# A cross-attention and mixture-of-experts kernel: expert loop bounds read from the table once, a table of steps of its own for the first batch, and the low half of the context split in two pieces

## The reference, cut to what matters

```python
# x: (8, 512, 256), ctx: (8, 1024, 256); 8 heads of 64, 8 experts, all float32
x = x + tanh(g_xattn) * attention(layernorm(x), ctx)
#   q = x @ Wq; k, v = ctx @ Wk, ctx @ Wv; softmax(q k^T / 8) @ v; @ Wo + bo
h = layernorm(x).reshape(4096, 256)
p = softmax(h @ router.T); top 2 of 8 experts, their weights normalised
keep the 1280 heaviest assignments of each expert, renormalise
x = x + tanh(g_ffn) * sum over kept experts of weight * ((h @ W1) * silu(h @ Wg)) @ W2
```

## Time and profile before

| what | value |
|---|---|
| time, median of 3 runs (lowest to highest) | 1725.2 us (1725.16 to 1726.33) |
| profiled execution, its own time | 1727.69 us |
| its span | 1726.0 us |
| TensorE busy | 1642.6 us, 95% |
| VectorE busy | 1270.0 us, 74% |
| ScalarE busy | 1050.0 us, 61% |
| GpSimd busy | 671.9 us, 39% |
| batch 0, first scores to those of batch 1 | 21.78 to 153.85 us |
| search, TensorE's part (slot 4) | 1145.7 to 1149.0 us |
| experts 1 to 7 | 1196.48 to 1715 us |

### The profile page before, as it was taken

The page is one execution under the profiler, slowest core; times in us unless marked ns, Lnnn a source line. Parts: engine busy times, 40 slices in busy tenths (PEclk is TensorE's granted clock), DMA queues, the critical chain, the costliest instruction groups (busy, mean ns, idle before and its releaser), DMA issues.

```text
span 1726.0 us, 33535 instructions
## 1 busy us (share of the span) xinstructions
PE 1642.6 (95%) x12454; PEld 1494.2 (87%) x12454; DVE 1270.0 (74%) x2595; ACT 1050.0 (61%) x2179; POOL 671.9 (39%) x615
## 2 busy tenths in 40 slices
PE   6999999999999999999999998999999999999997
PEld 4788878887888887888888886889999999999997
DVE  6887888888888888888888878676565556547443
ACT  5776766766767666766676766535454455546443
POOL 3342444444345345245345334423343422232322
PEclk9999999999999999999999999999999999999999
DMA  4200220121121021031030022314423421341212
GB/s 126 124 25 1 85 77 26 64 86 38 35 107 45 17 121 50 13 124 51 13 124 32 20 120 85 135 44 106 114 41 108 111 34 39 97 113 28 38 32 28
DMA packets 60555, 115.49 MB, mean 67 GB/s; under 512 B 6616, under 2 KB 48480, under 8 KB 59776
## 3 DMA queue, kind: packets, MB, share of 16 engines
q1 hardware_dynamic: 37104, 79.24, 13.0%
q0 software_dynamic: 15392, 18.66, 5.9%
q10 hardware_dynamic: 7920, 15.73, 2.6%
HBM read 90.27 MB, written 57.42 MB: 86 GB/s over the span
## 4 chain that ended last, share of the span: by engine, by line
PE 76%; DVE 11%; issue 4%; POOL 3%; ACT 3%; DMA 1%; POOLq 0%; DVEq 0%; SPq 0%; ACTq 0%
PE ring L1207 11%; PE turned L1101 11%; PE ffn L1064 10%; PE ffn L1066 10%; PE ffn L1065 10%; PE scores L1089 9%; DVE neg_max L1888 5%; PE ring L1064 4%; PE ring L1066 3%; PE ring L1065 3%; DVE pt_l L1665 2%; PE ring L1173 1%; PE ring L1175 1%; POOL lists L855 1%; POOL probs L889 1%
## 5 line engine op out<-in xcount | busy, mean ns | idle before, releaser
L889 POOL TENSOR_SCALAR probs<-probs,row_rec 128x1024 f32<-128x1024 f32 x254 | 282.2, 1123 | 478.6 <-DVE row_rec L1991 466.9
L1429 ACT ACTIVATE pt_h<-turned 128x512 fp32r<-128x512 f32 x512 | 279.5, 602 | 209.7 <-PE turned L1101 209.2
L1665 DVE TENSOR_TENSOR pt_l<-turned,pt_h 128x512 fp32r<-128x512 f32 x512 | 331.0, 680 | 7.2 <-ACT pt_h L1429 6.8
L1888 DVE TENSOR_REDUCE neg_max<-scores 128x1 f32<-128x1024 f32 x256 | 301.5, 1218 | 35.7 <-PE scores L1089 35.6
L1101 PE MATMUL turned<-ident,probs 128*128 128x128 f32 x2048 | 281.9, 279 | 30.3 <-DVE pt_l L1665 23.3
L1101 PEld LDWEIGHTS turned<-ident,probs 128*128 128x128 f32 x2048 | 224.2, 141 | 98.4 <-issue 69.9
L1485 ACT ACTIVATE probs<-scores,neg_max 128x1024 f32<-128x1024 f32 x256 | 285.3, 1117 | 14.9 <-DVE neg_max L1888 14.8
L1207 PE MATMUL ring<-pt_h,v_hl 128*128 128x256 f32 x1024 | 261.4, 293 | 0.2
L1207 PE MATMUL ring<-pt_l,v_hl 128*128 128x256 f32 x1024 | 250.9, 283 | 0.0
L2256 DVE TENSOR_TENSOR act_f<-ffn,silu 128x256 f32<-128x256 f32 (+1 forms) x232 | 108.4, 467 | 130.7 <-ACT silu L1599 123.3
L1207 PEld LDWEIGHTS ring<-pt_h,v_hl 128*128 128x128 f32 x1024 | 195.7, 191 | 4.0 <-issue 1.9
(11 more groups left out here) (258 smaller groups left out, 3905.4 us busy)
## 6 DMA issues: line engine op xcount, KB each, us to landing
lists<-pads SPq DMA_DIRECT2D x8, 4160.0 KB
w_raw<-w_t ACTq DMA_DIRECT2D x10, 1024.0 KB, 8.3
e_rows<-lists SPq DMA_DIRECT2D x26, 390.0 KB
ctx_raw<-ctx_t SPq DMA_DIRECT2D x15, 512.0 KB, 3.8
wg_raw<-wg_t ACTq DMA_DIRECT2D x5, 1024.0 KB, 7.8
x_in<-x SPq DMA_DIRECT2D x8, 512.0 KB, 4.0
x_sum<-x SPq DMA_DIRECT2D x8, 512.0 KB, 4.0
out<-x_sum SPq DMA_DIRECT2D x8, 512.0 KB, 2.9
```

Source lines behind the costliest of these rows:

```text
L889: nc.gpsimd.tensor_scalar(probs[:, k, :], probs[:, k, :], row_rec[:, k:k + 1], 1.0, ALU.mult, ALU.mult).then_inc(scaled, 1)
L1429: return nc.scalar.activation(dst, src, ACT.Copy)
L1665: return nc.vector.tensor_tensor(dst, src, hi_part.bitcast(F32), ALU.subtract)
L1888: nc.vector.tensor_reduce(neg_max[:, k:k + 1], scores[:, n % 2, :].rearrange("p (a c) -> p a c", a=2), AX.XY, ALU.max, negate=True).then_i ...
```

## The change

Four edits, in a diff cut to its core.

TensorE no longer loads bounds at each expert. The search loads, right after it has waited for the table, two ends for each of the experts 1 to 7 (14 loads) ahead of the one of the turns; VectorE computes the wide ends (row 2) and a copy of the ends (row 6) in two more small operations. The other engines load as before. `FIRST` has a table of its own, `FIRST_JOBS`, and `FIRST_EARLY` says for each even step how many of the two `low_turned` stand between the two `highest`. GpSimd's `ctx_l` is written as two operations of 128x512 instead of one of 128x1024. `FILL_A` keeps later tiles where they were.

```diff
-FILL_A = 32
+FILL_A = 24
+FIRST_JOBS = {
+    0: [("w", 1, 0), ("k", 1, 0)],
...
+    7: [("k", 2, 0)],
+    8: [("v", 1, 0)],
...
+FIRST_EARLY = {0: 2, 2: 2, 4: 1, 8: 2, 12: 2, 14: 1, 16: 1, 18: 1, 22: 1, 24: 1, 28: 1, 30: 1}
-LOW_BETWEEN = (24, 26, 28, 30)
+LAST_EARLY = {24: 2, 26: 2, 28: 2, 30: 2, UNITS - 1: 2}
...
-FIRST = Body(0, False, True, True, START.end - RING, START)
+FIRST = Body(0, False, True, True, START.end - RING, START, FIRST_JOBS)
...
-                nc.gpsimd.tensor_tensor(ctx_l[:, :, part], ctx_raw[:, :, :],
-                                        ctx_h[:, :, part].bitcast(F32), ALU.subtract)\
-                    .then_inc(ctx_split, 1)
+                for kc in range(KC):
+                    last = nc.gpsimd.tensor_tensor(ctx_l[:, kc, part], ctx_raw[:, kc, :],
+                                                   ctx_h[:, kc, part].bitcast(F32), ALU.subtract)
+                last.then_inc(ctx_split, 1)
...
                     pe.wait_ge(table_done, 1)
+                    for e in range(1, E):
+                        ends.append([pe.value_load(table[0:1, row, e:e + 1], min_val=LEAST_MORE,
+                                                   max_val=MOST_CHUNKS) for row in (2, 6)])
                     turns = pe.value_load(table[0:1, 3, 1:2], min_val=1, max_val=WEIGHT_BITS)
...
-                wides = pe.value_load(table[0:1, 4, ds(e, 1)], min_val=1, max_val=2)
-                chunks = pe.value_load(table[0:1, 0, ds(e, 1)], min_val=1, max_val=T // CHUNK)
-                before = pe.value_load(table[0:1, 1, ds(e, 1)], min_val=0, max_val=MOST_CHUNKS)
+                wide_end, end = ends[e - 1]
...
-                with pe.Fori(0, wides) as j:
-                    whole_chunk(pe.snap(before + j), parity, WT)
-                with pe.Fori(0, chunks) as j:
-                    whole_chunk(pe.snap(before + wides + j), parity, ST)
+                with pe.Fori(start, wide_end) as n:
+                    whole_chunk(n, parity, WT)
+                with pe.Fori(wide_end, end) as n:
+                    whole_chunk(n, parity, ST)
+                return end
...
+                    nc.vector.tensor_tensor(table[:, 2, :], table_f[:, 1, :], table_f[:, 0, :], ALU.subtract)
+                    nc.vector.tensor_copy(table[:, 6, :], table_f[:, 1, :])
```

More of the change, by code:

```diff
@@ L109 @@
 FIRST_VALUES = {0: [("v", 0, 0), ("v", 0, 1)], 1: [("v", 0, 2)], 2: [("v", 0, 3)]}
+FIRST_JOBS = {
+    0: [("w", 1, 0), ("k", 1, 0)],
+    2: [("w", 1, 1)],
+    3: [("k", 1, 1)],
+    4: [("w", 1, 2), ("q", 1, 0)],
+    6: [("w", 1, 3)],
+    7: [("k", 2, 0)],
+    8: [("v", 1, 0)],
+    9: [("v", 1, 1)],
+    10: [("q", 2, 0)],
+    12: [("k", 2, 1)],
+    13: [("h", 0, 0)],
+    14: [("v", 1, 2)],
+    15: [("w", 0, 0)],
+    16: [("w", 0, 1), ("k", 3, 0)],
+    17: [("v", 1, 3)],
+    18: [("h", 1, 0)],
+    19: [("w", 0, 2), ("l", 0, 0)],
+    20: [("k", 3, 1), ("q", 3, 0)],
+    22: [("x", 0, 0)],
+    23: [("w", 0, 3), ("x", 1, 0)],
+    24: [("v", 0, 0), ("k", 0, 0)],
+    26: [("k", 0, 1)],
+    27: [("v", 0, 1), ("r", 0, 0)],
+    28: [("v", 0, 2), ("q", 0, 0)],
+    30: [("v", 0, 3)],
+}
+FIRST_EARLY = {0: 2, 2: 2, 4: 1, 8: 2, 12: 2, 14: 1, 16: 1, 18: 1, 22: 1, 24: 1, 28: 1, 30: 1}
 LN_STEPS = 6
@@ L173, in of @@
     def of(self, b):
-        return Body(b, self.prev, self.own, self.nxt, self.offset, self.before)
+        return Body(b, self.prev, self.own, self.nxt, self.offset, FIRST if b == 1 else self.before)
     def route_from(self):
@@ L319, in build @@
         table_f = tile(moe, "table_f", [P, 7, E])
-        table = tile(moe, "table", [P, 6, E], I32)
+        table = tile(moe, "table", [P, 7, E], I32)
         tile(moe, "rest_of_x_in", [P, FILL_A])
@@ L1238, in _ @@
             batches(pe, run)
+            ends = []
             def search(slot):
@@ L1402, in first_expert, with expert @@
                 down(pe.snap(chunks + EARLY - 1), FC - 1, 0)
[L1404 to L1408 removed]
+                return chunks
+            def expert(e, parity, start):
+                wide_end, end = ends[e - 1]
                 if e == 1:
                     pe.wait_ge(w_split, 2 * PIECES)
[L1412 to L1415 removed]
+                with pe.Fori(start, wide_end) as n:
[3 more added lines that the diff above has]
+                return end
             chunk(0, 0, True)
[L1418 removed]
+            start = first_expert()
             for e in range(1, E):
[L1420 removed]
+                start = expert(e, e % 2, start)
         @block.scalar
@@ L1960, in step @@
                     jobs = body.results(u)
-                    lows = body is LAST and u in LOW_BETWEEN + (UNITS - 1,)
-                    late = [(what, c) for what, c in jobs if lows and what[0] == "r"]
+                    done = 0
+                    if body.own and u >= 2:
+                        done = {FIRST: FIRST_EARLY, LAST: LAST_EARLY}.get(body, {}).get(u, 0)
+                    late = [(what, c) for what, c in jobs if body is LAST and done and what[0] == "r"]
                     jobs = [job for job in jobs if job not in late]
@@ L1969, in step @@
                         highest(b, u)
-                        if lows:
-                            low_turned(b, u - 2, 0)
-                            low_turned(b, u - 2, 1)
+                        for j in range(done):
+                            low_turned(b, u - 2, j)
                         if body is LAST and u == UNITS - 2:
@@ L1995, in step @@
                     between(body, u, 2)
-                    if (body.prev if u < 2 else body.own) and not lows:
+                    if (body.prev if u < 2 else body.own) and done < 1:
                         low_turned(b, u - 2, 0)
-                        between(body, u, 3)
+                    between(body, u, 3)
+                    if (body.prev if u < 2 else body.own) and done < 2:
                         low_turned(b, u - 2, 1)
-                    else:
-                        between(body, u, 3)
                     between(body, u, 4)
```

## The result

The changed kernel takes 1724.0 us (median of 16 runs, 1721.5 to 1725.7) beside 1726.3 for the kernel before on the same chip (median of 16); the ratio of the two is 0.9982, 95% interval 0.9975 to 0.9989: 0.18% or 3.1 us faster (1.9 to 4.3), at the edge of what can be told from no change. I had forecast 1719.4. The profiled execution of the change took 1722.29 us of its own (span 1720.6), 5.4 less than that of before, where my sum said 6.9.

A forecast was written before the change was run, and what follows sets the result against it. TensorE, at work 95% of the span, was taken as the bound, so only its idle time could yield gains. Terms -8.2 + 5.2 + 2.6 + 0.2 - 3.4 - 2.2 gave -5.8 against 1725.2: 1719.4 us, range 1711.5 to 1727.

The forecast's parts named there:

- The loads that go (-8.2): At the first matmul of experts 1 to 7, TensorE's idle time for bound loads should vanish: -8.2 us.
- nothing of the 8.24 us should stay: Claim that all seven issue gaps at experts 1 to 7 end, as one load and the branch are hidden.
- The loads that come (+5.2): In the search, 15 loads in a row at 0.6 us each bring the small matmul 5.2 us later.
- the rival of cheap loads: Loads cost 0.2 us each, so the search hides them, with no clock term: 1711.6 us; chance 0.12.
- The clock (+2.6): After over 8 us of standing still in the search, TensorE runs six microseconds at 1.2 GHz: +2.6 us.
- The table (+0.2): Two more small VectorE operations before `act_f`, for which TensorE waits ahead of the search: +0.2 us.
- Batch 0 (-3.4): New step order and early `low_turned` end TensorE waits in batch 0, less 0.6 for late maxima: -3.4 us.
- the wait of step 9: TensorE's 1.28 us wait in batch 0, expected to end because `pt_l` is ready 1.2 us sooner.
- I count nothing: In batch 0 steps with one `low_turned` moved, the second half of `turned` comes free as late as before: no gain.
- The two pieces (-2.2): VectorE gets in between two GpSimd `ctx_l` pieces in batches 1 to 6; two batches caught for the median: -2.2 us.
- 1.1 us for each batch that is caught: Where VectorE's L1748 meets GpSimd's `ctx_h`, two pieces let L1750 in at 254.8 instead of 255.9: 1.1 us.
- the four terms of the first edit: Moving the loads from experts to search: -8.2 for loads gone, +5.2 for loads added, +2.6 clock, +0.2 table.

The follow-up runs named there:

- e1: Kernel before with only the end loads moved into the search and the table's two more operations: 1727.2 us, ratio 1.0001.
- e6: The change with only the seven row ends loaded in the search and each wide end loaded at its expert: 1717.3 us, 0.9905 of the kernel before.
- e8: The change with batch 0 in the common table's order, low halves still early: 1727.0 us in one run.
- e16: Kernel before plus a small GpSimd memset ahead of the second half's `ctx_h`, so that it starts later: 1724.2 us, ratio 0.9955.
- e17: Kernel before plus a small VectorE memset ahead of L1748, so that it meets `ctx_h`: 1737.3 us, ratio 1.0036.
- e10: The change, unchanged, run again beside the kernel before on another chip: 1720.6 us, ratio 0.9906.
- e3: Kernel before with only the low half of the context written in two pieces: 1724.0 us, ratio 0.9985.
- e13: Second comparison of the kernel before with only the two context pieces: 1726.1 us, ratio 0.9984.
- e11: The change with its loads one at a time and the low context half in four pieces: 1713.7 us, 0.9863 of the kernel before.

## Why the prediction was right and wrong

**The loads that go (-8.2).** Right: none of the seven gaps is left. From expert 1's first matmul to the last of all, the change took 6.2 us less and e1 6.8, where the six gaps inside that stretch make 6.93. The change shows a wait of 1.02 us for `silu` in this stretch, at 1484.17, which neither e1 nor the kernel before has, so a part of the gaps came back as another wait; my "nothing of the 8.24 us should stay" left that out.

**The loads that come (+5.2).** Right in kind, a little small: 5.6 in the first profile, 0.64 us for a load (e6) against my 0.6. The Trainium skill gives a floor of about 600 ns for a `tensor_load` ("DMA: Bandwidth & Descriptors", Latency and other measured facts), and about 200 ns for a register load from HBM even in bulk ("Runtime: NRT & Kernel Launch", Instruction fetch mechanics); 0.64 us speaks for the first and against the second here, and with it the rival of cheap loads falls.

**The clock (+2.6).** 2.0 us against the profile of before, 1.8 to 2.7 in the five others. Against other kernels with the wait of 2.98 us it is less, since there that wait lowered the clock in eleven profiles of eleven, for 1.5 to 2.7 us, and only in the kernel before, in two of two, it did not. Why not there is open. So the first edit gained 0 against the kernel before and 1.4 against its like, and I had said 0.2.

**The table (+0.2).** Right as a term. The 2.0 us lost ahead of the search in the first profile came with ScalarE's late `silu`; why that was late is not settled. No term of mine stood for it. I can't say how many of the 16 runs had it.

**Batch 0 (-3.4).** Right in size, 3.0, and wrong in its reasons. The early halves alone gained 0.1 and not 2.2, and the wait of step 9, which was to end, grew. Of the 1.18 us at the second transpose x, 0.67 stayed. And "I count nothing" where one `low_turned` is moved was wrong in the old order (e8), where the second half is waited for at step 15 and 1.1 us of what was gained before is given back.

**The two pieces (-2.2).** Here a step failed: the count of caught batches. The "1.1 us for each batch that is caught" was right to 0.05 us, and in the pair of profiles batches 1 to 6 together took 3.2 us less, against -3.3. But the term was that price times a fixed number of caught batches, three in the profile and two for the median, the same for both kernels, since "the change does not touch that". The number is not fixed: 0, 0, 1, 3, 3 and 3 of six in six profiles with one operation, 0 to 3 in ten profiles with two pieces. The price is not fixed either, 2.0 or 3.5 us with one operation by whether the clock falls, and a catch still costs 0.95 with two pieces. With a small operation more that rules catches out, the kernel before takes 1724.2 us (e16), with one that forces all six 1737.3 (e17), and its median stood from 1726 to 1737 on its own. Catches make most of its spread there: with them ruled out its runs lie within 2.9 us, beside 15.5 on the same chip.

How many batches were caught in the 16 runs of the two kernels stays open, since only one execution of each was profiled. An estimate: the median of the kernel before is 1.35 us under its profile, which has three caught batches, and that of the change 1.73 us over its profile, which has two. At 2.05 and 0.95 us for a batch, and if nothing else moved the runs, that makes 2.3 and 3.8 caught, and a term of -1.1 (3.6 less 4.7) in place of -2.2. But something else does move them: e16, with no batch caught in its profile, has its median 1.4 us over that profile.

**The sum.** The pair of profiles can be counted in full. The change took 3.0 us less in batch 0 (forecast 3.4) and 3.2 less in batches 1 to 6 (3.3). From the transposes of the assignments to the last matmul it took 1.6 more, 578.2 instead of 576.6, where the four terms of the first edit made -0.2; 2.0 of that is the late `silu`. The rest of the 5.4 us, 0.8, lies at the start, in batch 7 and at the end. So there each price was right within 0.7 us by the readings above, and what was missing was a term for ScalarE. In the medians the gain was smaller still, 2.3 us (3.1 by the ratio). The late `silu` and the catches as estimated would make 3.1 of the 3.5 us between 2.3 and my 5.8; that is argued and not shown. Beside a kernel before at 1737 the same change gained 16 us (e10): it was worth between 3 and 16 us, and neither end was my 5.8.

## What to carry to other kernels

A profile shows one draw. Where two engines meet by hundredths of a microsecond, read the length of every repetition, price both outcomes, and then force each outcome by a small operation on one side; the better one can be kept, and was worth more here (e16: 0.45%) than the edit that softens the meeting (e3 and e13, on another chip: 0.16%). Register loads at one place add up at 0.64 us each and starve TensorE and then its clock; the same loads one at a time between matmuls cost nothing. Edits to a schedule are not additive: jobs moved without the early halves, or those without the jobs, gave 1.1 and 0.1 us of 3.0.

## What was unexpected of the hardware

- A VectorE operation with two SBUF operands that starts a few hundredths of a microsecond behind a GpSimd operation that reads and writes SBUF, or in the same hundredth, in most cases waits for all of it: 1.06 to 1.09 us behind `ctx_h`, in the rows shown of e11, e17 and the change. Where it is at work ahead of `ctx_h` it takes 0.18 (e16; 0.02 us ahead in the kernel before), and in batch 5 of the change too, where both start at 778.80. A memset of GpSimd, which reads nothing, did not hold it (e16, 253.34). The Trainium skill says that the two engines share SBUF interfaces, and names contention with VectorE instructions that have two SBUF inputs ("GPSIMD Engine Reference", Key points); the rows agree.
- The same idle time of TensorE did or did not lower its clock: 1.61 us in e17 lowered it in two batches of six, 2.98 us in the search in eleven profiles of thirteen. A stretch at 1.2 GHz behind a short wait cost 1.4 to 1.5 us.
